# Four buffers for the experts' gathered rows and results, a larger table of unread rows, and a later table load for the last curve

## What is computed

```python
xn = _layernorm(x)
# attention: 8 heads, each of two softmax maps whose weighted difference is taken
attn = jax.nn.softmax(scores + causal)            # (b, 16, s, s)
attn = attn[:, :nh] - attn[:, nh:] * lmbda
out = attn @ v                                    # then RMS norm in groups of 4, times (1 - L_INIT)
s = out @ wo.T
# experts: E = 8, top 2 of 8 for each of 4096 tokens
logits = h @ router_weight.T + router_bias
top_w = jax.nn.softmax(top_k(logits, 2))
glu = gate * sigmoid(gate * 1.702);  act = (up + 1.0) * glu
out = sum over the two experts of top_w * (act @ down_proj[e] + bias[e])
x = x + s * silu(out)
```

## Time and profile before

| what | before |
|---|---|
| median of 3 runs | 1023.85 us (1023.36 to 1024.76) |
| the profiled execution: its own time | 1022.34 us |
| its span, first to last instruction | 1020.6 us |
| PE, DVE, ACT, POOL busy, share of the span | 89%, 87%, 75%, 28% |
| mean granted TensorE clock | 0.978 |
| first matmul of the span starts at | 12.40 us |
| expert block, first gather to last scatter | 743.84 to 975.77 us |

### The profile page before, as it was taken

The page is one execution under the profiler, slowest core; times in us unless marked ns, Lnnn a source line. Parts: engine busy times, 40 slices in busy tenths (PEclk is TensorE's granted clock), DMA queues, the critical chain, the costliest instruction groups (busy, mean ns, idle before and its releaser), DMA issues.

```text
span 1020.6 us, 23981 instructions
## 1 busy us (share of the span) xinstructions
PE 907.0 (89%) x6614; PEld 641.3 (63%) x6614; DVE 886.8 (87%) x1743; ACT 768.3 (75%) x2011; POOL 283.0 (28%) x481
## 2 busy tenths in 40 slices
PE   4999985889989899989988898898879999999987
PEld 3877763666666666666666666666646665555676
DVE  6687867999999999999999999999848887778847
ACT  3545435999999999999999999999835555464443
POOL 3000001323332333333200000001146666656610
PEclk9999995999999999999999999999989999999999
DMA  6989966485667758575685556474013333333278
GB/s 209 334 317 314 288 249 187 100 190 139 144 153 173 166 116 185 140 149 139 141 109 125 122 106 141 86 151 92 7 54 120 113 113 99 107 97 106 79 229 287
DMA packets 89553, 157.54 MB, mean 154 GB/s; under 512 B 19580, under 2 KB 48764, under 8 KB 89468
## 3 DMA queue, kind: packets, MB, share of 16 engines
q1 hardware_dynamic: 80544, 137.56, 52.2%
q0 software_dynamic: 8960, 19.41, 6.3%
HBM read 104.57 MB, written 52.36 MB: 154 GB/s over the span
## 4 chain that ended last, share of the span: by engine, by line
PE 33%; DVE 23%; ACT 13%; issue 12%; ACTq 1%; another core or an unknown queue 0%; DVEq 0%; DMA 0%; POOL 0%; POOLq 0%
PE bank L1461 11%; DVE Pr_long L1241 7%; DVE nmax L1191 7%; PE bank L1021 6%; PE bank L1487 5%; ACT Pr_long L1124 4%; DVE nmax L1209 4%; ACT Pr_short L1138 4%; ACT AT L1151 3%; PE bank L1062 2%; PE bank L1528 2%; PE bank L1447 1%; PE bank L1474 1%; PE bank L1023 1%; DVE nmax L1203 1%
## 5 line engine op out<-in xcount | busy, mean ns | idle before, releaser
L1191 DVE TENSOR_REDUCE nmax<-bank 128x1 f32<-128x1024 f32 (+3 forms) x256 | 259.9, 1015 | 5.8 <-PE bank L1023 5.8
L1124 ACT ACTIVATE Pr_long<-bank,nmax 128x1024 f32<-128x1024 f32 (+3 forms) x256 | 252.2, 985 | 9.9 <-DVE nmax L1191 9.8
L1151 ACT COPY AT<-bank 128x512 f32<-128x512 f32 (+3 forms) x384 | 177.3, 494 | 4.3 <-PE bank L1062 2.4
L1021 PE MATMUL bank<-Ks_first,Qs_first 128*128 128x512 f32 (+3 forms) x384 | 123.9, 412 | 28.1 <-ACT Pr_short L1138 18.6
L1138 ACT ACTIVATE Pr_short<-bank,nmax 128x128 f32<-128x128 f32 (+3 forms) x256 | 138.5, 541 | 10.1 <-DVE nmax L1209 2.6
L892 POOL COPY VO<-Ob 128x64 f32 (+1 forms) x128 | 30.2, 236 | 414.3 <-ACT Ob L1160 413.9
L1062 PE MATMUL bank<-ident,Pr_long 128*128 128x128 f32 x832 | 127.9, 280 | 18.3 <-DVE Pr_long L1241 18.2
L1461 PE MATMUL bank<-gu_sb,xsT 128*128 x284 | 135.8, 601 | 4.5 <-ACT xsT L1549 2.7
L1021 PE MATMUL bank<-Ks_second,Qs_second 128*128 128x512 f32 (+3 forms) x384 | 119.2, 399 | 20.7 <-ACT Pr_short L1138 18.5
L1241 DVE SCALAR_TENSOR_TENSOR Pr_long<-Pr_long,coef 128x1024 f32<-128x1024 f32 (+3 forms) x128 | 137.4, 1074 | 0.0
L1023 PE MATMUL bank<-maskb,identb 128*128 128x128 bf16 x512 | 117.8, 233 | 0.0
(11 more groups left out here) (171 smaller groups left out, 1607.3 us busy)
## 6 DMA issues: line engine op xcount, KB each, us to landing
q_parts<-PARTS SPq DMA_DIRECT2D x32, 512.0 KB, 3.1
k_parts<-PARTS SPq DMA_DIRECT2D x32, 512.0 KB, 3.9
Qs_first<-q_parts SPq DMA_DIRECT2D x64, 256.0 KB
Ks_first<-k_parts SPq DMA_DIRECT2D x64, 256.0 KB
Qs_second<-q_parts SPq DMA_DIRECT2D x64, 256.0 KB
Ks_second<-k_parts SPq DMA_DIRECT2D x64, 256.0 KB
X<-x SPq DMA_DIRECT2D x8, 512.0 KB, 5.6
xn_dram<-XN SPq DMA_DIRECT2D x8, 512.0 KB, 6.5
```

What stands on the lines that cost most here:

```text
L1021: nc.tensor.matmul(at[:, c0:c1], Qs[head][:, m, q * P:(q + 1) * P], Ks[head][:, m, c0:c1], start=True, stop=(c1 < N))
L1124: nc.scalar.activation(long_probs(p)[:, m, 0:N], long_slot[m][:, 0:N], ACT.Exp, bias=nmax[:, 4 * p + m:4 * p + m + 1], scale=1.0, accum_ou ...
L1151: nc.scalar.copy(AT[u % 6][:, 0:w], tb[u % BANKS][:, 0:w]).then_inc(unit_out, 1)
L1191: nc.vector.tensor_reduce(nmax[:, 4 * p + m:4 * p + m + 1], long_slot[m][:, 0:N], AX.X, ALU.max, negate=True).then_inc(long_maxed, 1)
```

## The change

`ROW_BUFS = 4` replaces the two buffers of `xs` and of `ys`, each with its own semaphore, and `AHEAD` goes from 5 to 7. The two loads of `ys` at the start go away, and the waits count from zero. `y_dram` gets `4 * P` unread rows instead of `2 * P`, so the iota table `no_rows` has 18 partitions of 8192 numbers instead of 36 of 4096, and it is written, with `row_ids`, behind the other constants on POOL instead of ahead of eleven of them. The silu of one number stands behind the first three `turned_out` instead of ahead of them.

```diff
-AHEAD = 5
+AHEAD = 7
...
+ROW_BUFS = 4
-Y_ROWS = TOP_K * T + 2 * P
+Y_ROWS = TOP_K * T + ROW_BUFS * P
...
-            no_rows = sb("no_rows", [SLOT_TILES // 2, 2 * P, ID_WORDS], I32, where=ph)
+            no_rows = sb("no_rows", [SLOT_TILES // ROW_BUFS, ROW_BUFS * P, ID_WORDS], I32, where=ph)
...
                     nc.gpsimd.tensor_copy(identb[:], ident[:]).then_inc(consts_done, 1)
-                    nc.gpsimd.iota(no_rows[:], pattern=[[1, 2 * P], [0, ID_WORDS]], base=TOP_K * T, channel_multiplier=0
-                                   ).then_inc(no_rows_ready, 1)
-                    nc.gpsimd.iota(row_ids[:], pattern=[[P, NT], [T, TOP_K]], base=0, channel_multiplier=1
-                                   ).then_inc(no_rows_ready, 1)
...
                     nc.gpsimd.tensor_scalar(count_128, count_f[:, 0:T // P], float(P), None, ALU.mult
                                             ).then_inc(consts_done, 1)
+                    nc.gpsimd.iota(no_rows[:], pattern=[[1, ROW_BUFS * P], [0, ID_WORDS]], base=TOP_K * T, channel_multiplier=0
+                                   ).then_inc(no_rows_ready, 1)
+                    nc.gpsimd.iota(row_ids[:], pattern=[[P, NT], [T, TOP_K]], base=0, channel_multiplier=1
+                                   ).then_inc(no_rows_ready, 1)
...
                     def rows_in(n):
-                        pool.wait_ge(xs_turned, seen(n // 2 - 1, n % 2))
-                        pool.indirect_dma_start(xs[n % 2][:], None, xn_dram, bass.IndirectOffsetOnAxis(
-                            slot_tokens[:, n:n + 1], 0)).then_inc(xs_loaded[n % 2], 16)
+                        if n >= ROW_BUFS:
+                            pool.wait_ge(xs_turned, 2 + n - ROW_BUFS + 1)
+                        u = n % ROW_BUFS
+                        pool.indirect_dma_start(xs[u][:], None, xn_dram, bass.IndirectOffsetOnAxis(
+                            slot_tokens[:, n:n + 1], 0)).then_inc(xs_loaded[u], 16)
...
-                    for u in range(2):
-                        pool.dma_start(ys[u][:], xn_dram[0:P, :]).then_inc(y_stored[u], 16)
-                    for n in range(2, AHEAD):
+                    for n in range(1, AHEAD):
                         rows_in(n)
...
-
-                    nc.scalar.activation(silu_table[:], ident[:, 0:1], ACT.Silu)
                     for c in range(W_SETS):
                         turned_out(c)
+
+                    nc.scalar.activation(silu_table[:], ident[:, 0:1], ACT.Silu)
                     for c in range(NCH):
...
-                    nc.vector.wait_ge(y_stored[u], 16 * (it + 1))
-                    nc.vector.tensor_tensor(ys[u][:], ybank[u][:, 0:D],
+                    m = 2 * it + u
+                    if m >= ROW_BUFS:
+                        nc.vector.wait_ge(y_stored[m % ROW_BUFS], 16 * (m // ROW_BUFS))
+                    nc.vector.tensor_tensor(ys[m % ROW_BUFS][:], ybank[u][:, 0:D],
```

More of the change, by code:

```diff
@@ L222, in load_head @@
                 sp.dma_start(K[g * DH:(g + 1) * DH, :, :].bitcast(F32), kp).then_inc(qk_loaded[u], 16)
-        xs_loaded = [sem(f"xs_loaded{u}") for u in range(2)]
+        xs_loaded = [sem(f"xs_loaded{u}") for u in range(ROW_BUFS)]
         consts_done = sem("consts_done")
@@ L1279, in build @@
         with ExitStack() as ph:
-            xs = [xs_first, sb("xs_second", [P, D], where=ph)]
+            xs = [xs_first] + [sb(f"xs{u}", [P, D], where=ph) for u in range(1, ROW_BUFS)]
             xsT = [sb(f"xsT{u}", [P, HC, P], where=ph) for u in range(2)]
@@ L1286, in build @@
             act_T = [sb(f"act_T{u}", [P, HC, P], where=ph) for u in range(2)]
-            ys = [sb(f"ys{u}", [P, D], where=ph) for u in range(2)]
+            ys = [sb(f"ys{u}", [P, D], where=ph) for u in range(ROW_BUFS)]
             norm = sb("norm", [P, NIT, NORMS], where=ph)
@@ L1324, in build @@
             y_weighted = sem("y_weighted")
-            y_stored = [sem(f"y_stored{u}") for u in range(2)]
+            y_stored = [sem(f"y_stored{u}") for u in range(ROW_BUFS)]
             squared = sem("squared")
@@ L1366, in _ @@
                         sp.dma_start(xr[c][:], x_v[c]).then_inc(xr_loaded, 16)
-                    for u in range(2):
-                        sp.wait_ge(y_stored[u], 16 * ((FULL_TILES + 1 - u) // 2 + 1))
+                    for u in range(ROW_BUFS):
+                        sp.wait_ge(y_stored[u], 16 * len(range(u, FULL_TILES, ROW_BUFS)))
                     for c in range(NCH):
@@ L1388, in results_out @@
                         pool.indirect_dma_start(y_dram, bass.IndirectOffsetOnAxis(slots[:, n, 1:2], 0),
[L1389 to L1396 removed]
+                                                ys[n % ROW_BUFS][:], None).then_inc(y_stored[n % ROW_BUFS], 16)
+                    for n in range(1, AHEAD):
                         rows_in(n)
@@ L1401, in _ @@
                         results_out(n)
-                    for u in range(2):
-                        pool.wait_ge(y_stored[u], 16 * ((FULL_TILES + 1 - u) // 2 + 1))
+                    for u in range(ROW_BUFS):
+                        pool.wait_ge(y_stored[u], 16 * len(range(u, FULL_TILES, ROW_BUFS)))
                 def expert_loader(eng):
@@ L1598, in weigh @@
                         act.wait_ge(y_ready, seen(m // 2, m % 2))
-                        nc.scalar.activation(ys[m % 2][:], ys[m % 2][:], ACT.Copy, scale=slot_weights[:, m:m + 1]
+                        y = ys[m % ROW_BUFS]
+                        nc.scalar.activation(y[:], y[:], ACT.Copy, scale=slot_weights[:, m:m + 1]
                                              ).then_inc(y_weighted, 1)
```

13 lines of the change are left out of this document (5 added, 8 removed).

## The result

The changed kernel took 1030.61 us in the median of 4 runs (1026.82 to 1032.19), the kernel before 1023.61 (1021.98 to 1024.76, 4 runs beside them): ratio 1.0064, 95% interval 1.0033 to 1.0096. That is slower, as forecast, but outside the range of 1018.5 to 1029.0. The profiled execution took 1026.82, the shortest of the four, with a span of 1025.1. Of all executions on these pages, one of `n5_scatter_first` (1056.38 us, mean granted clock 0.842) and one of `g_four_late_3` (2864.28 us) were slow ones and are left out of medians, ranges and ratios.

The account below looks back on a forecast made before the run. It took the start to be one chain held by POOL's iota, then PE's pace of 3.02 us per tile and in the last part; +5.3 - 1.2 - 1.5 = +2.6 on 1023.85 gave 1026.45 us, range 1018.5 to 1029.0.

Parts of the forecast that it names:

- 1029.0, which is +4.1 with 1 us over it: Whole kernel: the range's upper end, set 1 us above the +4.1 case where the clock falls all the same.
- The iotas, +5.3: Start: the 8192-number iota, now behind the constants, holds L430 until 15.8, so PE gets its rows 5.3 us later.
- All that is behind ... moves with it: Behind the first normalising: split weights, split rows and projection hang on this chain in order and shift by its +5.3 us.
- Theory D: An experiment's expectation: a late start is partly made good by the phase in which blocks begin; 0 to +1 us.
- Four buffers, 0: Expert block: more buffers save nothing, because PE's completion was late and not the scatter; 0 us, bounds -3.5 to +0.5.
- The bound of -3.5: Expert block: the most that four buffers could gain, if the stalls called remote go; 3.5 us in 2 places.
- the buffers do cure the late completions: Rival, expert block: scatter in flight and ys guard share in the remote stalls; -3.5, total 1022.95; chance 0.13 with other oversights.
- The table load and the clock, -1.2 and -1.5: Last part: copies ahead of the table load cut PE's pause by 1.2 us; the clock mostly staying up saves 1.5.
- the rival in which the clock falls all the same: Rival, last part: the 1.5 us clock gain fails, +5.3 - 1.2 = +4.1, 1027.95 us; chance 0.28.
- The sum: Whole kernel: +5.3 - 1.2 - 1.5 = +2.6 on the median 1023.85, giving 1026.45 us.
- the faster rival: Start: L430 gets in ahead of the iota; with the table load 1018.1 to 1019.6 us; chance 0.17.
- The rival of the slipping L430: Start: L430 precedes the iota, nothing is held, normalising ends 3.1 us earlier; -5.8 in all, -4.3 without clock; chance 0.17.

Follow-up runs that it names:

- n5_scatter_first: The four-buffer kernel with the late iota, complete, each tile's scatter issued ahead of the gather seven tiles further on; 0.9955 of before.
- g_four_late_3: The changed kernel plus a wait holding the big iota until the first rows are normalised, unshifted and complete, rerun on another chip; 1012.28 us, 0.9929 of before.
- after: The changed kernel as first measured against the kernel before; median 1030.61 us, ratio 1.0064.
- g_four_early: The changed kernel as it is (four buffers, long iota ahead of the first x), rerun in the two-by-two on one chip; 1.0034 of before.
- after_again: The changed kernel unchanged, measured again on another chip; 1.0003 of before.
- t1_table: The kernel before with only the table load moved behind the first three chunks' copies; ratio not stated, its interval includes 0.9974; last part 42.9 us.
- g_two_early: The changed kernel with xs, ys and AHEAD as before (two buffers), in the two-by-two; the same kernel stood at 1.0026 of before on an earlier chip.
- s1_order: The kernel before with only both iotas moved behind the small tables, still 4096 numbers per partition; +2.3 us, with 2.4 to each side.
- q_before_plain: The kernel before with plain stores in place of the scatters, output left out; runs include 1014.08 and 1021.38 us, as fast as before.
- n1: The four-buffer kernel with the late iota, without the 71 scatters and without the gathers from the fifth tile on; 0.9865 of before.
- n2: The four-buffer kernel with the late iota, without the 71 scatters but with all gathers; 0.9845 of before.
- a1_late_iota: The changed kernel plus one wait: POOL begins the big iota only after DVE has normalised the first rows; 0.9952 of before.

## Why the prediction was wrong

**The step that failed** is what the range allowed for everything outside the edits: "1029.0, which is +4.1 with 1 us over it", together with "a measurement of this kernel can tell about 0.2%, 2.05 us". One profiled execution, with 3.5 us of remote waits, stood for the expert block on both sides: "0 us", with bounds of -3.5 and +0.5. The runs show in its place: the block takes 224.3 to 234.5 us in fourteen executions, and the same changed kernel stood at +6.6, +0.3 and +3.5 us to before. The interval of the first comparison alone has 3.2 us to each side. The terms of the start and of the last part hold within 0.4 us in the profiles, and the buffers' 0 within 1.6 us in the medians.

**The iotas, +5.3: mechanism right, 4.96 measured.** Iota from 6.95 for 8.66 us (7.1 and 8.7 forecast), the `tensor_scalar` L430 of before held for 8.34 (8.4), first matmul 17.36 (near 17.6). "All that is behind ... moves with it" is right too, but the bare stages hide it. At the first gate and up product the six kernels with an 8192 iota ahead of x are at 750.3 to 752.9, mean 751.4, before and the two others with its start at 746.8 to 748.4, mean 747.6: +3.7 only. Most of the difference to 4.96 is the granted clock near 135 us. Windows from 130 to 140 (us, busy of PE, PEld, DVE, ACT and POOL, PEclk, DMA share, GB/s), before:

```profile
130.00:140.00 10.00, 7.21 (x27) 5.39 (x28) 3.96 (x14) 3.54 (x8) 0.00 (x0) 0.83 1.00 381
```

the changed kernel in `after`:

```profile
130.00:140.00 10.00, 7.38 (x36) 5.49 (x34) 9.14 (x28) 3.83 (x8) 0.00 (x0) 1.00 1.04 354
```

and the same changed kernel in `g_four_early`:

```profile
130.00:140.00 10.00, 7.38 (x30) 5.56 (x29) 8.20 (x27) 3.39 (x7) 0.00 (x0) 0.86 1.04 370
```

In before the granted clock stands at the lower level (0.50) for a part of these 10 us, and the product at 132.45 takes 3.66 us. In `after` the same product takes 2.02, in `g_four_early` 3.57. PE's rows of this product and of the next of its kind, in before, `after` and `g_four_early`:

```profile
132.45 3.66 PE L722 MATMUL bank<-wv_sb,XNT 128*128 128x264 f32 x8 [1.24 <-DVE logits L511]
137.54 3.87 PE L722 MATMUL bank<-wv_sb,XNT 128*128 128x264 f32 x16 [1.44 <-ACT XNT L635]
...
138.29 2.02 PE L724 MATMUL bank<-wv_sb,XNT 128*128 128x264 f32 x8 [1.24 <-DVE logits L513]
141.74 3.87 PE L724 MATMUL bank<-wv_sb,XNT 128*128 128x264 f32 x16 [1.44 <-ACT XNT L637]
...
137.38 3.57 PE L724 MATMUL bank<-wv_sb,XNT 128*128 128x264 f32 x8 [1.24 <-DVE logits L513]
142.39 3.87 PE L724 MATMUL bank<-wv_sb,XNT 128*128 128x264 f32 x16 [1.44 <-ACT XNT L637]
```

So the lower clock belongs to the execution and not to the shifted start: one and the same code had it in `g_four_early` and not in `after` and `after_again`. (Theory D, by which a late start is spared it, falls by this.) Compared with like, the shift arrives whole. With a mean clock of 0.91 from 125 to 145 us, attention begins at 162.03 and 162.10 in before and `t1_table` and at 166.88 and 167.36 in `g_four_early` and `g_two_early`: +5.05. With 1.00, it begins at 166.07 to 166.31 for the long iota ahead of x and at 157.81 to 158.28 for the late one: 8.1, which is near the 8.0 to 8.2 of the first matmul. At the first gate and up product `t1_table` is at 746.79 and the two at 751.45 and 752.11: +4.7 and +5.3 (before, at 747.72, had met the lower level once more near 737 us). All three profiles with before's start had the lower clock there and only two of the six with the changed start; whether that is chance stays open.

**Four buffers, 0: right.** Four pairs give -0.23, -0.03, +0.03 and +0.09%. The bound of -3.5 and the rival "the buffers do cure the late completions" fall: the blocks with four have as many late completions (9 to 31) as those with two (15 to 28). The reading of the earlier trace rows was right that PE's completion was late and not the scatter. It stopped one question short: what makes them late, and how much they are in another execution. From 760 to 960 us DVE's bias add waits for "remote" 3.5 us in 2 places in before, 4.3 in 3 in `after`, and not once in `after_again`, which is the same code.

**The table load and the clock, -1.2 and -1.5: right in size.** The last part takes 45.6, 46.7 and 45.6 us in the three profiles with the load ahead of the copies (before, `s1_order` and `q_before_plain`; first product 5.16, 5.59 and 5.08), and 42.7 to 43.0 in fifteen of the seventeen with it behind (3.62 in each): -2.7. In the other two, `n1` and `n2`, it takes 46.2 and 46.0, with the pause as short as in the fifteen. The timeline of `n1` has the transposes ahead of the pause slow already, 1.97 us where they take 1.09 in before:

```profile
966.12 1.97 PE L1517 MATMUL bank<-ident,VO 128*128 128x128 f32 x8 [0.63 <-DVE ys L1686]
968.85 1.94 PE L1517 MATMUL bank<-ident,VO 128*128 128x128 f32 x8 [0.77 <-ACT OnT L1624]
970.59 5.48 PE L1527 MATMUL bank<-wo_sb,OnT 128*128 128x256 f32 x16
```

So the rival in which the clock falls all the same (+4.1) exists, but there the clock fell ahead of the pause and not behind it, and it did not happen in the changed kernel's three profiles. By the rule of the Trainium skill (TensorE: Matmul & The Clock Gate, "What's actually happening") the observation of the clock runs free of the kernel, and the 1.5 us would come in some executions and not in others. Fifteen of seventeen had them, and the two others are kernels without scatters; no run shows the 1.5 us missing behind a pause in a complete kernel.

**The sum.** Start and last part say +5.0 - 2.7 = +2.3 where I had +2.6; the plain means of the stages say +3.7 - 2.7 = +1.0. The changed kernel was measured at 1.0064, 1.0003 and 1.0034, that is +6.6, +0.3 and +3.5 us. The forecast lies between them, and the first comparison lies 1.6 us above its range; counted from their own runs of before, the second and the third lie inside it. Whether the range held was thus in part a matter of luck. Some 4 us of the first comparison's +6.6 stay open: in its profile 4.0 of them are in the expert block, but four runs on either side, in a kernel whose block varies by 10 us, cannot tell chance from a property of that chip. Two sizes in the prediction are off without weight: the middle of the faster rival is 1018.8 and not 1018.5, and 8192 numbers at 4.38 / 4096 are 8.76 us and not 8.7.

**The rival of the slipping L430** did not happen as such, but `a1_late_iota` made it happen with one wait: first matmul at 9.38 (-3.1 forecast for that start, -3.02 found), where nothing of the chain is held. In five comparisons such kernels stand at 0.993 to 0.996 of before, ahead of both.

## What to carry to other kernels

Two instructions on two engines, an iota of 8.66 us and a `tensor_scalar` on four numbers, cost 8 us by their order alone; the long instruction goes behind the first chain that everything hangs on, with a wait, not ahead of it and not left to a race of 0.35 us. Before a change that is worth some us is forecast, ask how much the block it sits in varies from one execution to the next: waits that the profile calls remote, or completions that two engines see late together, say that one profile does not price that block, and the range must hold that. And a stretch that comes out shorter in one profile than in another can be the granted clock of that execution: look at a second execution of the same code before it is put down to an edit. Whether it pays to make one of two indirect transfers per tile plain stays open: no completion was late then, but the time stood at 1.0001 of before, and at 0.9913 beside 0.9929.

## What was not expected of the hardware

- Completions of PE arrived up to 2.5 us behind the modelled end, in groups. With two indirect transfers per tile there were 9 to 31 of them in each of fourteen profiles, with one, none, or one plain and one indirect, none were late in six.
- A `tensor_scalar` on 128x4 stood 3.21, 3.90 and 8.34 us for iotas of 4.38, 4.38 and 8.66 us, and ended 0.02 to 0.03 us behind each. By the Trainium skill (SBUF — State Buffer, "Who interferes with whom") this is the exclusion of a two-port `tensor_scalar` by GpSimd for the whole instruction; these rows agree. The same page's other case agrees too: a `tensor_tensor` took 0.16 in the midst of the write-only iota.
- The granted clock near 135 us differed between executions of one and the same code: mean 0.86 from 130 to 140 us in `g_four_early`, 1.00 in `after` and `after_again`. The product there took 3.57 us against 2.02.
- An iota's time went by the numbers in a partition and not by the partitions: 36x4096 took 4.38 us and 18x8192 took 8.66.
